# Turning attention rows with VectorE and SBUF transfers instead of TensorE transposes

## The chip, the cores and the metric

The kernel runs on one core of one Trainium2 chip. The metric is the device time in microseconds of one execution, taken as the median of the runs of a kernel. Inputs and outputs are float32. The kernel is one program with its instructions placed on the engines by hand: TensorE (PE), VectorE (DVE), ScalarE (ACT), GpSimd (POOL), and SyncE (SP), which issues all transfers.

## The reference, cut to what matters

One post-norm decoder layer on x of shape (4, 512, 512): a gated slot attention, a cross attention with a context of (4, 512, 128), and a gated feed-forward layer, each followed by a layer norm. The change touches the first of them alone. Each of its 16 heads has keys of 64, values of 128 and 64 slots:

```
q, k, v, g, s = x@Wq, x@Wk, x@Wv, x@Wg, clip(x@Ws, -32, 32)     # per head: 64, 64, 128, 128, 64
z  = cumlogsumexp(s) over time;  p = exp(s - z)
ok[t] = q[t] . sum_{u<=t} k[u] * decayed p[u]                   # a score for each slot
pv[t] = softmax(ok[t]) over the 64 slots
o[t]  = pv[t] . sum_{u<=t} decayed p[u] * v[u]
o = o * rsqrt(mean(o^2) + 1e-5) * g_norm_weight                 # over the 128 values
o = o * g * sigmoid(g)
x = layernorm(x + o.reshape(t, 16*128) @ Wo)
```

The kernel works with e = exp(s), the slot "probabilities" before they are divided by their running sum z, and multiplies by 1/z where it is needed. It needs e twice: with slots on partitions (`eT`, from the projection) and with time on partitions (`e`). It needs the output rows `og` with time on partitions (from the last products) and turned, with the 128 values of a head on partitions (`oT`), as the stationary operand of the product with Wo.

## The kernel before, in words

The attention walks 32 steps n = 4p + j: p is one of 8 pairs of heads, j one of 4 batch elements, each with 512 times in 4 tiles of 128. After 31 of them (n = 0 to 30, all built by one `step` function per engine) comes `last_step` (n = 31), then `output_and_max`, and then the cross attention and the feed-forward layer. Each engine has its own list of instructions, written out in order; engines meet by semaphores alone, so a wait holds up everything behind it on the same engine. TensorE's order sets the shape of a step. In step n it runs, one after the other: the three causal score chunks of n; the projections S and VG of step n+1 (each projection group is 12 matmuls of 512 columns: 4 parts of the inner dimension, 3 products of high and low halves); `slots(n)` (L1131) and `states(n)` (L1103); `out_rows(n)`, 8 transposes of the rows `og` that step n-1 left; the projection VG+1; 4 transposes of the normalised slot scores; `project_out(n)`, 24 matmuls that multiply the turned rows of step n-1 by Wo; 4 transposes of the slot softmax `pv`; the projections VG+2 and VG+3; the diagonal score blocks; the projections Q and K; `transpose_e(n + 1)`, 4 transposes; and `values(n)` (L1144, L1149). All transposes of this part go through `transpose4` and have line L1004 in the profile.

Around this, GpSimd works out the factors of the norm (`factor`) and multiplies the rows by them (`scale_o`, L808). ScalarE copies the turned rows out of PSUM as the rounded high half `oT_hi` (L1554), VectorE makes the low half `oT_lo` (L1820), both with the factor 0.5 times the norm's weight (`gw_half`). VectorE adds each product with Wo to `acc` (`add_out`, L1828), takes slot maxima (L1845), subtracts them (L1850), sums (L1856) and scales (L1860); ScalarE's exponential stands between (L1591). VectorE's `gated_output` (L1873) writes `og` at the end of a step. ScalarE copies the transposed probabilities to `e` (L1559).

SyncE holds only weight loads in this part (L556, L561, L564, L570), five at a time for the next pair and one for Wo. Projections wait for the `gate_ready` count of the projection two groups earlier, so VG+3 waits for the gating of VG+1, Q for that of VG+2. Every product is three matmuls of float32r halves (`mm3`, L66 to L68).

Of the kernel before, what the change touches and what calls it, by code (L numbers as in the profile page):

```python
# [147 lines left out]
def layer_program(nc, x, ctx_in, Wq, Wk, Wv, Wg, Ws, Wo, gw, gate_w, up_w, down_w, gate_s, up_s, down_s, out,  # L148
# [6 lines left out]
    with ExitStack() as ctx:  # L155
        place = {}

        def sb(name, shape, dt=F32):
            place[name] = (nc.sbuf_base + 31) // 32 * 32
            return ctx.enter_context(nc.sbuf_tensor("a_" + name, shape, dt))  # L160
# [5 lines left out]
        def sem(name):  # L166
            return ctx.enter_context(nc.semaphore("a_" + name))
# [24 lines left out]
        og = sb("og", [P, 2 * TT, DV])  # L192
# [5 lines left out]
        oT_hi = sb("oT_hi", [P, 2, T], F32R)  # L198
        oT_lo = sb("oT_lo", [P, 2, T], F32R)
# [51 lines left out]
        oT_done = sem("oT_done")  # L251
        wo_done = sem("wo_done")
# [42 lines left out]
        def each_pair(eng, step):  # L295

            for n in range(NSTEP - 1):
                step(n, n // B, n % B, n == 0)

        def at(n, k):  # L300

            return isinstance(n, int) and n == k
# [270 lines left out]
        def _(sp):  # L573
# [102 lines left out]
        def _(pool):  # L676
# [99 lines left out]
            def split_wo(p):  # L776
                pool.wait_ge(raw_wo_in, (p + 1) * 16)
                split(raw_wo, wo_hi[:, :, :], wo_lo[:, :, :], wo_hi_ready, wo_ready, p + 1)
# [25 lines left out]
            def scale_o(n):  # L804

                wait(pool, fac, FAC * n)
                wait(pool, og_ready, 2 * n)
                nc.gpsimd.tensor_tensor(og[:, :, :], og[:, :, :],  # L808
                                        f1[:, :].rearrange("p (g o) -> p g o", o=1).broadcast_to([P, 2 * TT, DV]),
                                        ALU.mult).then_inc(ogs_ready, 1)  # L810
# [45 lines left out]
            nc.gpsimd.tensor_scalar(gw_half[:, :], gw_half[:, :], 0.5, None, ALU.mult).then_inc(gw_ready, 1)  # L856
            split_wo(0)
# [66 lines left out]
        def _(pe):  # L924
# [182 lines left out]
            def out_rows(n):  # L1107

                wait(pe, ogs_ready, n)
                for h in range(2):  # L1110
                    transpose4(ob[h], [og[:, 2 * t + h, :] for t in range(TT)]).then_inc(oT_done, 1)

            def project_out(n, pair, tiles):

                pe.wait_ge(wo_ready, pair + 1)
                wait(pe, oTlo_ready, 2 * n)
                for t in tiles:
                    if t >= 2:
                        wait(pe, added, 4 * (n - 1) + t - 1)
                    for h in range(2):  # L1120
                        mm = mm3(pe, ob[t % 2], (oT_hi[:, h, t * P:(t + 1) * P], oT_lo[:, h, t * P:(t + 1) * P]),
                                 (wo_hi[:, h, :], wo_lo[:, h, :]), h == 0, h == 1)
                    mm.then_inc(wo_done, 1)
# [34 lines left out]
            def step(n, p, j, first):  # L1158
# [8 lines left out]
                pe.wait_ge(e_ready, n + 1)  # L1167
# [6 lines left out]
                if not first:  # L1174
                    out_rows(n)
# [8 lines left out]
                if at(n, 1):  # L1184
                    transpose_x(3, (0, 1))
                if not first:
# [7 lines left out]
                    if into:  # L1194
                        pe.wait_ge(opsT_ready, 1)
                        transpose_operands(0, 0, 2)
                pe.wait_ge(pv_ready, n + 1)
                transpose4(okb, [pv[:, 2 * t:2 * t + 2, :].rearrange("p h m -> p (h m)") for t in range(TT)])\
                    .then_inc(pvT_done, 1)
                if into:  # L1200
                    pe.wait_ge(opsT_ready, 2)
                    transpose_operands(0, 0, 3)
                next_project(VG + 2)
                if into:
                    pe.wait_ge(opsT_ready, 3)
                    transpose_operands(0, 0, 4)
                    pe.wait_ge(added, 4 * n)
                    max_pair(0, 0)
# [18 lines left out]
                transpose_e(n + 1)  # L1227
# [4 lines left out]
            def last_step(n):  # L1232
                pe.wait_ge(left_ready, 2 * n + 1)
                pe.wait_ge(right_ready, 2 * n + 1)
                pe.wait_ge(e_ready, n + 1)
# [253 lines left out]
        def _(act):  # L1489
# [60 lines left out]
            def copy_oT(n):  # L1550

                for h in range(2):
                    wait(act, oT_done, 2 * (n - 1) + h + 1)
                    nc.scalar.activation(oT_hi[:, h, :], ob[h], ACT.Copy,  # L1554
                                         scale=gw_half[:, 0:1]).then_inc(oThi_ready, 1)
# [17 lines left out]
            def step(n, p, j, first):  # L1573
# [11 lines left out]
                if not first:  # L1585
                    copy_oT(n)
# [5 lines left out]
                if into:  # L1592
                    copy_queries(0, 0, 1)
                    copy_queries(0, 0, 2)
                if at(n, 0) or at(n, 1):
                    high_x(n + 2)
                act.wait_ge(wT_ready, n + 1)
                high_right(wT)
                if into:
                    copy_queries(0, 0, 3)  # L1600
                next_proj(VG + 2)
                if into:
                    copy_queries(0, 0, 4)
# [3 lines left out]
                copy_e(n + 1)  # L1607
# [111 lines left out]
        def _(dve):  # L1719
# [97 lines left out]
            def low_oT(n):  # L1817
                for h in range(2):
                    wait(dve, oThi_ready, 2 * (n - 1) + h + 1)
                    nc.vector.scalar_tensor_tensor(out=oT_lo[:, h, :], in0=ob[h],  # L1820
                                                   scalar=gw_half[:, 0:1], in1=oT_hi[:, h, :].bitcast(F32),
                                                   op0=ALU.mult, op1=ALU.subtract).then_inc(oTlo_ready, 1)
# [43 lines left out]
            def gated_output(n, j):  # L1866
                ob = value_banks(n)
                for half in (1, 0):
                    if half:
                        dve.wait_ge(o_done, n + 1)  # L1870
                    else:
                        dve.wait_ge(sq_done, 2 * n + 1)
                    nc.vector.tensor_tensor(og[:, :, :].rearrange("p (t h) c -> p t h c", h=2)[:, :, half, :],  # L1873
                                            ob[half].rearrange("p (t c) -> p t c", c=DV),
                                            gate[:, j % 2, :, half * DV:(half + 1) * DV], ALU.mult).then_inc(og_ready, 1)

            def step(n, p, j, first):
# [17 lines left out]
                if at(n, 0) or at(n, 1):  # L1895
                    less_maxima(n)
# [6 lines left out]
                if not (at(n, 0) or at(n, 1)):  # L1903
                    less_maxima(n)
# [4 lines left out]
                slot_sum(n)  # L1909
                if not first:  # L1910
                    add_out(n, (j - 1) % B, (2, 3))
                scaled_weights(n)
                slot_reciprocals(n)
                dve.wait_ge(wT_ready, n + 1)
                low_right(wT, 2 * n + 1)
                if norm_now and not into:
                    statistics(n, j - 1)
                gating(n + 1, VG + 2, b1)
# [278 lines left out]
```

## Time and profile before

| | |
|---|---|
| runs of the kernel before | 1991.13, 1991.74, 1994.18 us; median 1991.74 |
| profiled execution, first to last instruction (its time on the page) | 1991.0 us |
| TensorE busy | 1963.5 us, 99% of the span |
| VectorE / ScalarE / GpSimd busy | 1367.6 / 780.5 / 562.7 us |
| attention steps, 30 to 1168 us | 1138 us, TensorE busy 1134 of them, granted clock 1.00 |
| mean granted TensorE clock | 0.995 |

The page adds up what each engine was busy with. It is one execution, a little under the median. Durations of matmuls overlap, because they are pipelined: what a matmul costs is the distance from its start to the next one's start, not its duration. A row of the timeline merges equal neighbours: it gives the start, the duration from the first start to the last end, engine, line, what is written and read, and how many. PEld is the load of the stationary operand, which runs beside the matmul before it. SPq is SyncE issuing a transfer; its duration is that of the issue, not of the transfer.

### The profile page before, as it was taken

How to read it: one execution, taken by the hardware profiler on the slowest of the kernel's cores; microseconds unless marked ns; L12 is line 12 of the kernel's file. 1: busy time of each engine (PE TensorE's matmuls, PEld its weight loads, DVE VectorE, ACT ScalarE, POOL GpSimd, SP SyncE). 2: the span in 40 equal slices, each digit the busy share in tenths (PEclk: the TensorE clock that was granted, in tenths of full speed). 3: DMA queues.
4: the chain of work that ended last, by engine and by line, in shares of the span. 5: the costliest groups of instructions: out<-in, count | busy, mean ns of one | idle time of the engine just before them, and what ended most of it. 6: DMA issues, size and time to landing. Idle time of an engine off the chain costs nothing.

```text
span 1991.0 us, 30723 instructions
## 1 busy us (share of the span) xinstructions
PE 1963.5 (99%) x11879; PEld 1444.2 (73%) x11879; DVE 1367.6 (69%) x2206; ACT 780.5 (39%) x1915; POOL 562.7 (28%) x600
## 2 busy tenths in 40 slices
PE   8999999999999999999999989999999999999998
PEld 7888888878878888888788874444444478888886
DVE  4666666666666666666666778999999865555556
ACT  3332232332332322323323324888888732122123
POOL 2142152152152242242242333244242211111112
PEclk9999999999999999999999998999999999999999
DMA  5000100100001001001000000111110100000002
GB/s 169 1 1 12 38 1 12 38 2 25 24 12 37 2 11 38 1 11 38 1 12 3 6 2 19 30 29 26 26 31 20 34 17 16 32 16 16 31 17 85
DMA packets 58449, 46.89 MB, mean 24 GB/s; under 512 B 14288, under 2 KB 47056, under 8 KB 58320
## 3 DMA queue, kind: packets, MB, share of 16 engines
q1 hardware_dynamic: 58320, 45.11, 7.7%
q8 instruction: 88, 1.44, 0.3%
q14 instruction: 41, 0.34, 0.1%
HBM read 32.78 MB, written 4.19 MB: 19 GB/s over the span
## 4 chain that ended last, share of the span: by engine, by line
PE 94%; ACT 3%; DVE 2%; issue 0%; DMA 0%; POOL 0%; POOLq 0%; DVEq 0%; SPq 0%; ACTq 0%
PE a_ps L66 20%; PE a_ps L68 19%; PE a_ps L67 19%; PE a_ps L988 6%; PE a_ps L950 5%; PE a_ps L1004 4%; PE a_ps L1131 4%; PE a_ps L1144 3%; PE a_ps L972 3%; PE a_ps L1064 2%; PE a_ps L932 2%; PE a_ps L1067 2%; PE a_ps L1070 2%; ACT x_prob L1651 2%; PE a_ps L1149 1%; PE a_ps L1103 1%
## 5 line engine op out<-in xcount | busy, mean ns | idle before, releaser
L1725 DVE TENSOR_REDUCE a_raw_qks<-a_ps 128x1 f32<-128x512 f32 x512 | 321.1, 684 | 16.8 <-PE a_ps L950 15.9
L1651 ACT ACTIVATE x_prob<-a_ps 128x512 f32<-128x512 f32 x512 | 280.7, 611 | 62.9 <-PE a_ps L972 61.4
L66 PE MATMUL a_ps<-a_vg_hi,a_xT_lo 128*128 128x512 f32 x512 | 205.0, 400 | 0.0
L68 PE MATMUL a_ps<-a_vg_hi,a_xT_hi 128*128 128x512 f32 x512 | 199.8, 390 | 0.0
L67 PE MATMUL a_ps<-a_vg_lo,a_xT_hi 128*128 128x512 f32 x512 | 199.6, 390 | 0.0
L1777 DVE SCALAR_TENSOR_TENSOR a_gate<-a_gate,a_ps 128x256 f32<-128x256 f32 x128 | 53.8, 420 | 180.1 <-ACT a_gate L1539 180.1
L783 POOL TENSOR_TENSOR a_causal<-a_causal,a_mask 128x128 f32<-128x128 f32 x32 | 14.7, 458 | 557.7 <-ACT a_causal L1544 557.7
L66 PE MATMUL a_ps<-a_xT_hi,a_qks_lo 128*128 128x512 f32 x384 | 157.5, 410 | 0.4 <-DVE a_xT_lo L1756 0.4
L890 POOL TENSOR_TENSOR f_h_lo<-f_h,f_h_hi 128x512 fp32r<-128x512 f32 x44 | 57.0, 1295 | 334.8 <-ACT f_h_hi L1686 334.8
L68 PE MATMUL a_ps<-a_xT_hi,a_qks_hi 128*128 128x512 f32 x384 | 150.5, 392 | 0.0
L67 PE MATMUL a_ps<-a_xT_lo,a_qks_hi 128*128 128x512 f32 x384 | 149.5, 389 | 0.0
L950 PE MATMUL a_ps<-a_xT_lo,a_xT_hi 64*128 64x512 f32 x384 | 143.4, 461 | 2.3 <-DVE a_raw_qks L1725 1.6
L972 PE MATMUL a_ps<-a_xT_hi,a_xT_lo 64*128 64x512 f32 x384 | 140.7, 452 | 0.6 <-ACT x_prob L1651 0.5
L66 PE MATMUL a_ps<-a_xT_hi,f_gu_lo 128*128 128x512 f32 x352 | 138.3, 393 | 0.0
L68 PE MATMUL a_ps<-a_xT_hi,f_gu_hi 128*128 128x512 f32 x352 | 137.1, 390 | 0.0
L67 PE MATMUL a_ps<-f_xT_lo,f_gu_hi 128*128 128x512 f32 x352 | 137.0, 389 | 0.0
L988 PE MATMUL a_ps<-x_prob,x_values 128*32 128x512 f32 x1024 | 137.0, 608 | 0.0
L950 PEld LDWEIGHTS a_ps<-a_xT_lo,a_xT_hi 64*128 64x128 f32 x384 | 61.2, 188 | 97.4 <-issue 38.8
L1537 ACT COPY a_v<-a_ps 128x256 f32<-128x256 f32 x128 | 47.8, 373 | 207.4 <-PE a_ps L68 207.4
L2053 DVE TENSOR_TENSOR acc<-acc,a_ps 128x512 f32<-128x512 f32 x172 | 115.5, 686 | 8.7 <-PE a_ps L68 8.7
L68 PEld LDWEIGHTS a_ps<-a_vg_hi,a_xT_hi 128*128 128x128 f32 x512 | 96.1, 188 | 20.3
L1828 DVE TENSOR_TENSOR acc<-acc,a_ps 128x512 f32<-128x512 f32 x128 | 87.9, 688 | 31.5 <-PE a_ps L68 23.8
(202 smaller groups left out, 4593.8 us busy)
## 6 DMA issues: line engine op xcount, KB each, us to landing
a_raw_vg<-in_L_attn_Wv_dram SPq DMA_DIRECT2D x8, 512.0 KB, 4.0
a_raw_vg<-in_L_attn_Wg_dram SPq DMA_DIRECT2D x8, 512.0 KB, 6.3
a_raw_qks<-in_L_attn_Wo_dram SPq DMA_DIRECT2D x8, 512.0 KB, 3.7
a_xT_lo<-a_xT_lo SPq DMA_DIRECT2D x32, 128.0 KB, 2.3
x_values<-acc SPq DMA_DIRECT2D x13, 256.0 KB, 2.8
acc<-in_x_dram SPq DMA_DIRECT2D x3, 1024.0 KB, 10.2
out_dram<-acc SPq DMA_DIRECT2D x6, 512.0 KB, 2.8
f_raw_down<-in_L_ffn_down_w_dram SPq DMA_DIRECT2D x11, 256.0 KB, 2.9
```

What stands on the lines that cost most here:

```text
L66: pe.matmul(out, w_lo, x_hi, start=start, stop=False)
L67: pe.matmul(out, w_hi, x_lo, start=False, stop=False)
L68: return pe.matmul(out, w_hi, x_hi, start=False, stop=stop)
L950: pe.matmul(max_bank(u, q, i, par), qs[q][HALF[par], tile, st * P:(st + 1) * P], ks[q][(tile // 2) ^ par][HALF[par], :], start=True, stop= ...
L972: pe.matmul(score_bank(q, s, par), ks[q][g ^ par][HALF[par], t * P:(t + 1) * P], qs[q][HALF[par], 2 * g + pair, :], start=True, stop=True) ...
L988: mm = pe.matmul(avb[32 * i:32 * (i + 1), :], cv[:, q, t, g, :], prob[i % 2][:, (s + i // 2) % 4, :], start=(t == 0), stop=(t == TT - 1))
L1004: last = pe.transpose(bank[:, i * P:(i + 1) * P], src, ident[:, :])
L1131: mm = pe.matmul(okb[DK * h:DK * (h + 1), i * P:T], e[:, i, DK * h:DK * (h + 1)], causal[:, h, KEY_AT[i]:KEY_AT[i] + T - i * P], start=(i ...
L1651: nc.scalar.activation(prob[par][:, s % 4, :], score_bank(q, s, par), ACT.Exp, scale=X_SCALE).then_inc(exp_done[par], 1)
L1725: nc.vector.tensor_reduce(nm[:, q % 2, i % 4, par, i // 4:i // 4 + 1], max_bank(u, q, i, par), AX.X, ALU.max, negate=True).then_inc(max_re ...
L1828: nc.vector.tensor_tensor(a, a, ob[t % 2], ALU.add).then_inc(added, 1)
L2053: nc.vector.tensor_tensor(a, a, down_bank(v, b, t), ALU.add).then_inc(f_added, 1)
```

## The change

Rows and probabilities are no longer turned by TensorE. For the output rows of steps n = 1 to 30, VectorE turns `og` (128x1024) inside its 32x32 blocks in one instruction (`turn_output`); then SyncE issues 16 transfers inside SBUF, each of a block of 32 partitions with 8 runs of 32 words on each, that put the blocks in their transposed places in `oT_raw` (`move_output`), which lies over `oT_lo`. ScalarE copies all of it to `oT_hi` once the 16 have landed (`high_turned`), and GpSimd makes `oT_lo` (`low_turned`). For the probabilities of steps 1 to 31, VectorE turns `eT` (128x512) in the same way into the first half of `og`'s words (`turn_e`), once the 16 transfers that read `og` have landed, and SyncE issues 16 more with 4 runs of 32 words on each partition (`move_e`). `gated_output` waits for these, since it writes `og`. TensorE loses 8 + 4 transposes of a step; steps 0 (for its own `e`), 31 and the last output keep theirs. The factor `gw_half` is now multiplied into Wo by GpSimd (one more 128x1024 instruction for each pair). TensorE's order in a step becomes: chunks, S, VG, slots, states, VG+1, transposes of the scores, VG+2, transposes of `pv`, `project_out` with all four tiles, VG+3, diagonals, Q, K, values. VectorE's order changes with it. The core of the diff (the index views of `og` and the declarations of semaphores are cut; `MOVES` is 16 x 16, `TURNED` is 30):

```diff
-            with sp.Fori(1, PAIRS) as p:
-                sp.wait_ge(wo_ready, p)
-                sp.wait_ge(vg_ready, p)
-                load_s(sp, p)
-                load_vgqk(sp, p)
-                load_output(sp, p)
+            def move_output(n):
+                sp.wait_ge(og_turned, n)
+                wait(sp, wo_done, 4 * (n - 1))
+                for r in range(4):
+                    for c in range(4):
+                        sp.dma_start(oT_raw[32 * c:32 * (c + 1), :, 32 * r:32 * (r + 1)],
+                                     og[32 * r:32 * (r + 1), c, :, :]).then_inc(oT_in, 16)
+            def move_e(m):
+                sp.wait_ge(e_turned, m)
+                sp.wait_ge(states_done, m)
+                for r in range(4):
+                    for c in range(4):
+                        sp.dma_start(e[32 * c:32 * (c + 1), :, 32 * r:32 * (r + 1)],
+                                     og_words[32 * r:32 * (r + 1), P * c:P * (c + 1)]
+                                     .rearrange("p (i r) -> p i r", i=TT)).then_inc(e_in, 16)
+            for n in range(NSTEP - 1):
+                p, j = n // B + 1, n % B
+                if n:
+                    move_output(n)
+                move_e(n + 1)
+                if j == 0 and p < PAIRS:
+                    sp.wait_ge(wo_ready, p)
+                    sp.wait_ge(vg_ready, p)
+                    load_s(sp, p)
+                    load_vgqk(sp, p)
+                if j == 3 and p < PAIRS:
+                    load_output(sp, p)
...
             def split_wo(p):
                 pool.wait_ge(raw_wo_in, (p + 1) * 16)
+                nc.gpsimd.tensor_tensor(raw_wo, raw_wo, gw_half[:, :].rearrange("p (k o) -> p k o", o=1).broadcast_to([P, 2, D]), ALU.mult).then_inc(wo_scaled, 1)
+                pool.wait_ge(wo_scaled, p + 1)
...
+            def low_turned(n):
+                pool.wait_ge(oThi_ready, oT_count(n))
+                nc.gpsimd.tensor_tensor(oT_lo[:, :, :], oT_raw[:, :, :], oT_hi[:, :, :].bitcast(F32), ALU.subtract).then_inc(oTlo_ready, 1)
             def step(n, p, j, first):            # GpSimd
                 if not first:
                     factor(n - 1)
                     scale_o(n)
+                    low_turned(n)
...
             def step(n, p, j, first):            # TensorE
-                pe.wait_ge(e_ready, n + 1)
+                if first:
+                    pe.wait_ge(e_ready, 1)
+                else:
+                    pe.wait_ge(e_in, MOVES * n)
                 states(n, j)
-                if not first:
-                    out_rows(n)
                 next_project(VG + 1)
...
+                next_project(VG + 2)
+                pe.wait_ge(pv_ready, n + 1)
+                transpose4(okb, [...pv...]).then_inc(pvT_done, 1)
                 if not first:
                     project_out(n, pair0, (0, 1))
                     project_out(n, pair0, (2, 3))
-                pe.wait_ge(pv_ready, n + 1)
-                transpose4(okb, [...pv...]).then_inc(pvT_done, 1)
-                next_project(VG + 2)
                 next_project(VG + 3)
...
-                transpose_e(n + 1)
                 values(n, j)
...
+            def high_turned(n):                  # ScalarE, between the copies of VG and of VG+1
+                act.wait_ge(oT_in, MOVES * n)
+                nc.scalar.copy(oT_hi[:, :, :], oT_raw[:, :, :]).then_inc(oThi_ready, 1)
...
+            def turn_output(n):                  # VectorE
+                dve.wait_ge(ogs_ready, n)
+                nc.vector.transpose(og_words, og_words).then_inc(og_turned, 1)
+            def turn_e(m):
+                dve.wait_ge(eT_ready, m + 1)
+                wait(dve, oT_in, MOVES * (m - 1))
+                nc.vector.transpose(og_words[:, 0:T]..., eT[:, :]...).then_inc(e_turned, 1)
             def gated_output(n, j):
+                if n < NSTEP - 1:
+                    dve.wait_ge(e_in, MOVES * (n + 1))
...
             def step(n, p, j, first):            # VectorE
                 gating(n + 1, VG, b1)
+                if not first:
+                    turn_output(n)
                 normalised_slots(n)
                 running_states(n)
-                if not first:
-                    low_oT(n)
-                gating(n + 1, VG + 1, b1)
+                turn_e(n + 1)
                 slot_maxima(n)
+                less_maxima(n)
+                gating(n + 1, VG + 1, b1)
+                slot_sum(n)
+                scaled_weights(n)
+                slot_reciprocals(n)
+                if not at(n, 1):
+                    gating(n + 1, VG + 2, b1)
                 if not first:
                     add_out(n, (j - 1) % B, (0,))
+                dve.wait_ge(wT_ready, n + 1)
+                low_right(wT, 2 * n + 1)
                 if not first:
                     add_out(n, (j - 1) % B, (1,))
                 if not first:
                     add_out(n, (j - 1) % B, (2, 3))
```

## Rows read from the trace of the kernel before

**Rows 1.** the page, busy time of the engines, then the chain that ended last

```profile
PE 1963.5 (99%) x11879; PEld 1444.2 (73%) x11879; DVE 1367.6 (69%) x2206; ACT 780.5 (39%) x1915; POOL 562.7 (28%) x600
...
PE 94%; ACT 3%; DVE 2%; issue 0%; DMA 0%; POOL 0%; POOLq 0%; DVEq 0%; SPq 0%; ACTq 0%
```

**Rows 2.** a whole step: us; busy us and count by engine; clock; DMA share; GB/s

```profile
578.44:614.88 36.44, 36.44 (x236) 29.64 (x234) 22.36 (x35) 11.14 (x35) 11.62 (x11) 1.00 0.05 15
```

**Rows 3.** the timeline of TensorE in one step (start, duration, engine, line, what)

```profile
586.23 2.37 PE L1131 MATMUL a_ps<-a_causal,a_e 128*64 128x512 f32 x16
...
589.19 1.09 PE L1004 MATMUL a_ps<-ident,a_og 128*128 128x128 f32 x8
590.04 0.48 PE L66 MATMUL a_ps<-a_vg_hi,a_xT_lo 128*128 128x512 f32 x1
...
592.88 0.60 PE L1004 MATMUL a_ps<-ident,a_flat 128*128 128x128 f32 x4
593.24 0.47 PE L66 MATMUL a_ps<-a_wo_hi,a_oT_lo 128*128 128x512 f32 x1
...
598.81 0.60 PE L1004 MATMUL a_ps<-ident,a_flat 128*128 128x128 f32 x4
599.17 0.48 PE L66 MATMUL a_ps<-a_vg_hi,a_xT_lo 128*128 128x512 f32 x1
...
604.80 0.33 PE L1064 MATMUL a_ps<-a_right_hi,a_left_lo 64*128 64x128 f32 x2
...
611.88 0.60 PE L1004 MATMUL a_ps<-ident,a_eT 128*128 128x128 f32 x4
612.31 1.95 PE L1144 MATMUL a_ps<-a_v,a_causal 128*128 128x128 f32 x16
...
622.67 2.37 PE L1131 MATMUL a_ps<-a_causal,a_e 128*64 128x512 f32 x16
```

**Rows 4.** the timeline of GpSimd in the same step

```profile
585.90 1.90 POOL L808 TENSOR_TENSOR a_og<-a_og,a_f 128x1024 f32<-128x1024 f32 x1
...
589.73 2.40 POOL L759 TENSOR_TENSOR a_qks_lo<-a_raw_qks,a_qks_hi 128x1024 fp32r<-128x1024 f32 x1
```

**Rows 5.** the timeline of VectorE in the same step

```profile
587.03 0.42 DVE L1777 SCALAR_TENSOR_TENSOR a_gate<-a_gate,a_ps 128x256 f32<-128x256 f32 x1 [0.99 <-ACT a_gate L1539]
...
594.11 0.68 DVE L1845 TENSOR_REDUCE a_mx<-a_ps 128x8 f32<-128x512 f32 x1
...
607.60 1.22 DVE L1784 TENSOR_TENSOR_SCAN a_rz<-a_eT 128x512 f32<-128x512 f32 x1
```

**Rows 6.** the timeline of ScalarE in the next step, a copy from SBUF

```profile
618.15 0.70 ACT L1520 CAST a_left_hi<-a_eT 128x512 fp32r<-128x512 f32 x1
```

**Rows 7.** transfers issued back to back by SyncE inside SBUF

```profile
1200.67 1.10 SPq L618 DMA_DIRECT2D a_xT_lo<-a_xT_lo  x2
1201.88 0.67 SPq L609 DMA_DIRECT2D x_values<-acc  x1
```

**Rows 8.** a load from HBM, issued right behind another

```profile
349.42 0.46 SPq L561 DMA_DIRECT2D a_raw_vg<-in_L_attn_Wg_dram  x1
```

**Rows 9.** the page, transfers by size and median time from issue to landing

```profile
a_xT_lo<-a_xT_lo SPq DMA_DIRECT2D x32, 128.0 KB, 2.3
x_values<-acc SPq DMA_DIRECT2D x13, 256.0 KB, 2.8
```

**Rows 10.** queue, packets, MB, share of 16 engines: 1076 to 1084 us, two context loads

```profile
q1 hardware_dynamic: 1056, 0.13, 10.5%
```

**Rows 11.** the same for 1231 to 1236 us, runs of 2 KB inside SBUF

```profile
q1 hardware_dynamic: 160, 0.26, 23.2%
```

**Rows 12.** stretches around a wait of TensorE in the last step (columns as Rows 2)

```profile
1180.00:1185.00 5.00, 2.91 (x25) 2.29 (x26) 4.67 (x8) 2.15 (x4) 4.92 (x8) 0.98 0.00 0
1185.00:1190.00 5.00, 5.00 (x27) 4.30 (x27) 3.33 (x7) 0.00 (x0) 4.95 (x6) 0.50 0.09 15
1190.00:1195.00 5.00, 5.00 (x35) 4.40 (x35) 1.58 (x3) 1.58 (x13) 0.00 (x0) 0.84 0.01 2
```

More of the change, by code:

```diff
@@ L197, in layer_program @@
         squares = flat.rearrange("p (g c) -> p g c", c=DV).bitcast(mybir.dt.bfloat16)
-        oT_hi = sb("oT_hi", [P, 2, T], F32R)
-        oT_lo = sb("oT_lo", [P, 2, T], F32R)
+        oT_hi = sb("oT_hi", [P, 2 * TT, P], F32R)
+        oT_lo = sb("oT_lo", [P, 2 * TT, P], F32R)
+        oT_raw = over("oT_raw", "oT_lo", [P, 2 * TT, P])
         mask = sb("mask", [P, 5, P])
@@ L251, in layer_program @@
         oT_done = sem("oT_done")
+        og_turned = sem("og_turned")
+        oT_in = sem("oT_in")
+        e_turned = sem("e_turned")
+        e_in = sem("e_in")
+        wo_scaled = sem("wo_scaled")
         wo_done = sem("wo_done")
@@ L298, in each_pair, with oT_count @@
                 step(n, n // B, n % B, n == 0)
+        TURNED = NSTEP - 2
+        MOVES = 16 * 16
+        def oT_count(n, h=1):
+            return n if n <= TURNED else TURNED + 2 * (n - TURNED - 1) + h + 1
         def at(n, k):
@@ L1110, in out_rows @@
                 for h in range(2):
-                    transpose4(ob[h], [og[:, 2 * t + h, :] for t in range(TT)]).then_inc(oT_done, 1)
+                    transpose4(ob[h], [og_rows[:, 2 * t + h, :] for t in range(TT)]).then_inc(oT_done, 1)
             def project_out(n, pair, tiles):
                 pe.wait_ge(wo_ready, pair + 1)
-                wait(pe, oTlo_ready, 2 * n)
+                wait(pe, oTlo_ready, oT_count(n))
                 for t in tiles:
@@ L1120, in project_out @@
                     for h in range(2):
[L1121 removed]
+                        mm = mm3(pe, ob[t % 2], (oT_hi[:, 2 * t + h, :], oT_lo[:, 2 * t + h, :]),
                                  (wo_hi[:, h, :], wo_lo[:, h, :]), h == 0, h == 1)
@@ L1166, in step @@
                 pe.wait_ge(right_ready, 2 * n + 1)
-                pe.wait_ge(e_ready, n + 1)
+                if first:
+                    pe.wait_ge(e_ready, 1)
+                else:
+                    pe.wait_ge(e_in, MOVES * n)
                 into = n == NSTEP - 2
@@ L1185, in step @@
                     transpose_x(3, (0, 1))
+                next_project(VG + 2)
+                pe.wait_ge(pv_ready, n + 1)
+                transpose4(okb, [pv[:, 2 * t:2 * t + 2, :].rearrange("p h m -> p (h m)") for t in range(TT)])\
+                    .then_inc(pvT_done, 1)
                 if not first:
@@ L1585, in step @@
                 if not first:
-                    copy_oT(n)
+                    high_turned(n)
                 next_proj(VG + 1)
@@ L1599, in step @@
                 if into:
[L1600 to L1603, printed above, removed]
+                    for i in range(1, TILES):
+                        copy_queries(0, 0, i)
                 next_proj(VG + 3)
@@ L1818, in low_oT @@
                 for h in range(2):
[L1819 to L1822, printed above, removed]
+                    dve.wait_ge(oThi_ready, oT_count(n, h))
+                    nc.vector.tensor_tensor(oT_lo[:, :, :].rearrange("p (t h) c -> p h t c", h=2)[:, h],
+                                            ob[h].rearrange("p (t c) -> p t c", c=P),
+                                            oT_hi[:, :, :].bitcast(F32).rearrange("p (t h) c -> p h t c", h=2)[:, h],
+                                            ALU.subtract).then_inc(oTlo_ready, 1)
+            def turn_output(n):
[4 more added lines that the diff above has]
+                wait(dve, oT_in, MOVES * (m - 1))
+                nc.vector.transpose(og_words[:, 0:T].rearrange("p (s i r) -> p s i r", s=4, i=TT),
+                                    eT[:, :].rearrange("p (i s r) -> p s i r", i=TT, s=4)).then_inc(e_turned, 1)
             def add_out(n, b, tiles):
@@ L1872, in gated_output @@
                         dve.wait_ge(sq_done, 2 * n + 1)
-                    nc.vector.tensor_tensor(og[:, :, :].rearrange("p (t h) c -> p t h c", h=2)[:, :, half, :],
-                                            ob[half].rearrange("p (t c) -> p t c", c=DV),
-                                            gate[:, j % 2, :, half * DV:(half + 1) * DV], ALU.mult).then_inc(og_ready, 1)
+                    if n < TURNED:
+                        out = og[:, :, :, :].rearrange("p b (t h) r -> p t h b r", h=2)[:, :, half, :, :]
+                    else:
+                        out = og_rows.rearrange("p (t h) (b r) -> p t h b r", h=2, b=4)[:, :, half, :, :]
+                    nc.vector.tensor_tensor(out, ob[half].rearrange("p (t b r) -> p t b r", t=TT, b=4),
+                                            gate[:, j % 2, :, half * DV:(half + 1) * DV]
+                                            .rearrange("p t (b r) -> p t b r", b=4), ALU.mult).then_inc(og_ready, 1)
             def step(n, p, j, first):
```

57 lines of the change are left out of this document (25 added, 32 removed).

## The prediction, made before the changed kernel was run

> **What bounds the kernel now.** Read the page first: TensorE is busy for 1963.5 of 1991.0 us, and 94% of the chain that ended last is TensorE [rows 1]. A whole attention step then shows it more sharply: 36.44 us, TensorE busy in all of them at a granted clock of 1.00, VectorE for 22.36, ScalarE 11.14, GpSimd 11.62, the transfer engines at a share of 0.05 [rows 2]. So an instruction taken from TensorE shortens a step by its distance to the next start, and a new wait of TensorE lengthens it. The third view is TensorE's timeline of one step [rows 3], which gives these distances and the times at which it comes for its operands. From there it is a question of when the other engines deliver, read from their timelines. I work in the absolute times of the step that is shown; it repeats every 36.44 us (586.23 to 622.67, [rows 3]).
>
> **What goes.** The 8 transposes of the rows take 589.19 to 590.04, 0.85 us; the 4 of the probabilities 611.88 to 612.31, 0.43 us [rows 3]. The first go in steps 1 to 30, the second 31 times: 30 x 0.85 + 31 x 0.43 = 38.8 us. That is all that TensorE can gain.
>
> **When TensorE will want what is late now.** Without the row transposes VG+1 starts at 589.19 and ends 2.84 later (590.04 to 592.88), 592.03. The score transposes take 0.36, to 592.39. VG+2 takes half of 599.17 to 604.80, 2.82, to 595.21. There it wants `pv`; its transposes take 0.36 (598.81 to 599.17), and at 595.57 it wants both halves of `oT`. This is 2.33 us later than now (593.24). All from [rows 3].
>
> **When the rows arrive.** It is one serial chain.
> - GpSimd scales the rows until 585.90 + 1.90 = 587.80 [rows 4]. VectorE is free by then (587.03 + 0.42 = 587.45, [rows 5]).
> - VectorE's turn of 128x1024 words: the trace has no transpose on VectorE. An elementwise instruction took 0.42 for 256 columns and 0.68 for 512 [rows 5], so 0.26 for each 256 more: 0.68 + 2 x 0.26 = 1.2. The dearest per column that is near is the scan, 1.22 for 512 [rows 5], so 2.4. I take 1.2, since nothing says that it runs slower than one pass. With the handover it ends at 589.1.
> - 16 transfers, issued one after the other by one queue. The trace has none of 32 partitions. Inside SBUF, issues behind each other are (1201.88 - 1200.67) / 2 = 0.60 apart, and one takes 0.67 by itself [rows 7]; a load from HBM takes 0.46 [rows 8]. I take 0.60, the nearest in kind: the last is issued 15 x 0.60 = 9.0 after the first, at 598.15. It lands 2.3 later (2.8 for the 256 KB one, [rows 9]): 600.45.
> - Do the transfer engines keep up? 1056 packets, nearly all of 128 bytes, were 10.5% of 16 x 8 us, 13.4 us, so 13 ns each [rows 10]. A transfer here is 256 of them and 16 for the semaphore, 17 on each of 16 engines: 0.22 us, under 0.60. So the issue binds, not the bytes.
> - ScalarE's copy of 128x1024: 0.70 for 512 [rows 6], 1.3 for twice that (1.4 at most): 601.8.
> - GpSimd's difference of 128x1024: 2.40 for the same shape [rows 4]: with handovers 604.3.
>
> TensorE wanted it at 595.57: it waits 8.7 us. The output projection was moved by 2.33 us, the arrival by 11.
>
> **What else hangs on the 16.** `turn_e` waits for them on VectorE, and behind it stand the slot maxima, their subtraction, all gatings from VG+1 on, and the additions. 600.45, then the turn of 512 words 0.7, two instructions of 0.68 [rows 5], ScalarE's exponential about 0.70 [rows 6], handovers 0.2: `pv` comes at 603.4, where TensorE wants it at 595.21. So TensorE stands from 595.21, and this wait lies inside the longer one (604.3) with 0.5 us to spare after its 4 transposes. On ScalarE `high_turned` holds the two short copies of VG+1 and the exponential; it is done at 601.8, and the exponential is not asked for before 602.6. On GpSimd `low_turned` holds `split_qk` of the fourth step of a pair (4.3 us, to 608.6); Q starts at 604.3 + 5.57 + 2.82 + 1.48 = 614.2, so it is hidden by 5.6 us. The scaling of Wo, 1.9 us for a pair, is wanted a step later: nothing.
> - SyncE: free at 598.75; `turn_e` ends at 601.2, 16 more issues and a landing, 11.3 us, 612.5. The next step's chunks and `gated_output` want them near 624 (the step's start 578.44, [rows 2], plus 45.7). Hidden by 11 us; 32 issues are 19 us of a queue that is used for about 3 us a pair now. The weight loads queue behind them, with a step or more of slack. If the first 16 were quick and only these slow, nothing would be lost.
> - VectorE loses 1.4 us of `low_oT` and gains 1.9 of turns: nothing, it is not the bound.
>
> **The clock.** TensorE ran every step shown at 1.00. In the last step it had stood idle for 2.09 of 5 us, and the clock then was 0.50 (1.2 GHz) for 0.2 + 5 + 1.6 = 6.8 us, during which TensorE was busy throughout [rows 12]. A wait of 9 us in each step should do the same. While TensorE waits, the half clock costs nothing; I take about half of such a stretch, 3.6 us, to fall after the wait, and half speed loses half of it: 1.8 us a step. Bounds: 0 (it never falls, or is back in time), and 6.8 / 2 = 3.4.
>
> **The sum.** A step with a wait: -1.28 + 8.7 + 1.8 = +9.2 us, to 45.7. Thirty of them: +276.6; step 0 loses 0.43. Against the profiled 1991.0 us this is 2267 us; that execution lies 0.7 under the median of the runs, so I say 2268. Low end: issues 0.46 apart (-2.1) and no clock loss (-1.8), 3.9 x 30 = 117 less: 2150. High end: issues 0.67 and a landing of 2.8 (+1.5), VectorE's turn 2.4 (+1.2), clock 3.4 (+1.6), 4.3 x 30 = 130 more: 2397, widened to 2420 for the second rival.
>
> The Trainium skill, VectorE: DVE Perf Modes, section The three transpose paths, gives 311 ns for a 128x128 bf16 transpose in 32x32 blocks; no row shows one. Eight of these would be 2.5 us, an estimate by that page, and the sum would be 2306.
>
> **Rivals.**
> - *The transfers overlap as if they were one, and the kernel is faster.* For it: the bytes are small, 512 KB, and a single 256 KB transfer inside SBUF lands 2.8 us after its issue [rows 9]. The rows would be there at 592.0, both halves at 595.8, and TensorE would wait 0.2: 1991.0 - 38.8 + 6 = 1958. Place: SyncE's queue. It decides at an arrival 3.9 us after the turn, where the wait eats the 1.28; with 2.3 for the landing this wants issues (3.9 - 2.3) / 15 = 0.11 apart. Against it: no issue in [rows 7, 8] is under 0.46. The Trainium skill's rule says as much as this rival: DMA: Bandwidth & Descriptors, section Anatomy of one DMA, prices a transfer at 2.0 us plus bytes over 436 GB/s with setup and descriptors small; taken for 512 KB that is 3.2 us, and the kernel would take about 1970, an estimate by that page. The rule has no term for one queue issuing 16; the landing of 2.3 agrees with its fixed part. Chance 0.06.
> - *The packets bind.* If a packet of 128 bytes inside SBUF, from 32 partitions to 32 others, took as long as one of 2 KB there (23.2% of 16 x 5 us over 160 packets, 0.116 us, [rows 11]), a transfer would be 17 x 0.116 = 2.0 us, the sixteen 32 us in place of 9.6, and 30 steps 660 us more: up to 2930. Half of that extra is 2600. For it: no row has this kind. Against: the row for 128 bytes says a ninth. It decides from 0.60 / 17 = 35 ns a packet. Chance 0.08.
> - *The wait is there, the clock stays up*: 1.8 x 30 less, 2214. It lies inside the forecast's range.
> - *VectorE holds it up another way*, so that less is lost, or nothing changes: nothing on the page speaks for it. 0.04 in all, of which 0.01 within 0.2%.
>
> **Chances.** The forecast with its bounds 0.82, packets 0.08, overlap 0.06, the rest 0.04. The range 2150 to 2420 leaves out the overlap, most of the packets' case and some of the forecast's own tail. Within 0.2% (4 us) is about what a measurement of this kernel can't tell from no change. Faster 0.06, same 0.01, slower 0.93.
>
> **What would show it.** Right: a step of 44 to 47 us; SyncE's issues about 0.6 apart, 16 in a row twice a step; VectorE's line of `turn_e` waiting near 11 us for a transfer; TensorE idle for 8 to 9 us before the transposes of `pv` and `project_out`, and a granted clock under 1 in every step. Wrong: issues closer than 0.2, or `oT_lo` there when TensorE comes for it. If the wait is right but the clock stays at 1.00, only that term was wrong.

## The result, and the profile after

The changed kernel takes 2301.94 us (median of 4 runs, 2301.11 to 2303.61), the kernel before 1992.72 (1991.13 to 1994.18) on the same chip: a ratio of 1.156, 95% interval 1.154 to 1.157. Forecast were 2268 us and a range of 2150 to 2420: the direction and the mechanism came out, the size 34 us too small. The profiled execution has a span of 2299.4 us.

The page, busy time of the engines and the chain that ended last, as [rows 1]:

```profile
PE 1999.6 (87%) x11515; PEld 1454.8 (63%) x11515; DVE 1369.9 (60%) x2207; ACT 750.8 (33%) x1854; POOL 648.6 (28%) x638
...
PE 59%; SPq 12%; DVE 9%; POOL 8%; ACT 5%; issue 3%; DMA 3%; POOLq 0%; DVEq 0%; ACTq 0%
```

TensorE was 94% of the chain and is 59% now; the largest newcomer is SyncE's queue with 12%. A whole step, from one scaling of the rows on GpSimd to the next, as [rows 2]: 45.73 us where there were 36.44, TensorE busy for 37.12 of them, and a granted clock under 1.

```profile
674.49:720.22 45.73, 37.12 (x220) 29.59 (x219) 25.34 (x36) 10.28 (x33) 19.55 (x13) 0.93 0.12 18
```

The same step on each engine, to be read as one chain: first GpSimd and VectorE, as [rows 4, 5],

```profile
674.49 1.91 POOL L857 TENSOR_TENSOR a_og<-a_og,a_f 128x1024 f32<-128x1024 f32 x1
690.60 2.35 POOL L863 TENSOR_TENSOR a_oT_lo<-x_oT_raw,a_oT_hi 128x1024 fp32r<-128x1024 f32 x1 [14.20 <-ACT a_oT_hi L1610]
```

```profile
676.44 1.25 DVE L1877 STREAM_TRANSPOSE a_og<-a_og 128x1024 f32<-128x1024 f32 x1 [0.46 <-POOL a_og L857]
...
689.55 0.71 DVE L1882 STREAM_TRANSPOSE a_og<-a_eT 128x512 f32<-128x512 f32 x1 [10.45 <-DMA x_oT_raw<-a_og]
```

then the issues of SyncE, as [rows 7], and ScalarE, as [rows 6],

```profile
677.71 10.40 SPq L607 DMA_DIRECT2D x_oT_raw<-a_og  x16
690.29 10.83 SPq L616 DMA_DIRECT2D a_e<-a_og  x16
```

```profile
689.48 1.04 ACT L1610 CAST a_oT_hi<-x_oT_raw 128x1024 fp32r<-128x1024 f32 x1 [13.95 <-DMA x_oT_raw<-a_og]
...
691.60 0.63 ACT L1646 ACTIVATE a_flat<-a_flat 128x512 f32<-128x512 f32 x1 [0.52 <-DVE a_flat L1911]
```

and TensorE, as [rows 3]: behind VG+2 it stands for 8.33 us, until the exponential gives it `pv`. (The profile counts this from the modelled end of the last matmul, 683.56 + 0.39; counted from where the next one could have started, 683.56 + 0.23, it is 8.49.) Then come 4 transposes and the output projection, whose first starts are 0.43 apart where at full clock they are 0.23.

```profile
683.56 0.39 PE L68 MATMUL a_ps<-a_vg_hi,a_xT_hi 128*128 128x512 f32 x1
692.28 1.11 PE L1060 MATMUL a_ps<-ident,a_flat 128*128 128x128 f32 x4 [8.33 <-ACT a_flat L1646]
693.10 0.77 PE L66 MATMUL a_ps<-a_wo_hi,a_oT_lo 128*128 128x512 f32 x1
693.66 0.63 PE L67 MATMUL a_ps<-a_wo_lo,a_oT_hi 128*128 128x512 f32 x1
694.09 0.63 PE L68 MATMUL a_ps<-a_wo_hi,a_oT_hi 128*128 128x512 f32 x1
...
696.18 0.40 PE L67 MATMUL a_ps<-a_wo_lo,a_oT_hi 128*128 128x512 f32 x1
696.41 0.40 PE L68 MATMUL a_ps<-a_wo_hi,a_oT_hi 128*128 128x512 f32 x1
```

The waits of TensorE summed over the span (us in total, times, longest) show the two places that matter. One is the wait for `pv` in 29 steps; the other comes once, in step 30, 26.2 us in one piece, and the prediction did not have it.

```profile
PE a_ps L1060 <- ACT a_flat L1646: 242.4, 29, 9.5
PE a_ps L988 <- POOL a_raw_qks L761: 26.2, 1, 26.2
```

How that one comes about is on GpSimd's and SyncE's timelines. In step 30 GpSimd casts the operands of the cross attention, which TensorE turns ahead of VG+2. These casts now stand behind `low_turned`, and behind that GpSimd waits 9.05 us more for a context load, since SyncE issues that load only behind 16 + 16 moves.

```profile
1427.88 2.34 POOL L863 TENSOR_TENSOR a_oT_lo<-x_oT_raw,a_oT_hi 128x1024 fp32r<-128x1024 f32 x1 [14.18 <-ACT a_oT_hi L1610]
...
1440.10 2.04 POOL L734 TENSOR_TENSOR a_raw_vg<-acc,a_zero 128x512 fp32r<-128x512 f32 x2 [9.05 <-DMA a_raw_qks<-in_ctx_dram]
```

```profile
1415.01 10.39 SPq L607 DMA_DIRECT2D x_oT_raw<-a_og  x16
1427.57 10.24 SPq L616 DMA_DIRECT2D a_e<-a_og  x16
1437.86 1.14 SPq L651 DMA_DIRECT2D a_raw_qks<-in_ctx_dram  x2
```

The books by the starts of GpSimd's scaling: from n = 1 to n = 30 a step took 36.54 us on average before and 46.21 after, 29 x 9.66 = 280; the stretch from n = 30 to n = 31 43.3 before and 73.6 after, 30.3 more. That is 310 of the 308 us by which the spans differ.

### The profile page after: what moved, and what is told of

The parts are those of the page before. It is cut to its first block, busy times and chain, and to the rows that moved or that the text cites. A ratio compares the mean times of both kernels' runs of the same rounds, so it can differ in the third digit from the quotient of the medians.

```text
span 2299.4 us, 30948 instructions
## 1 busy us (share of the span) xinstructions
PE 1999.6 (87%) x11515; PEld 1454.8 (63%) x11515; DVE 1369.9 (60%) x2207; ACT 750.8 (33%) x1854; POOL 648.6 (28%) x638
## 4 chain that ended last, share of the span: by engine, by line
PE 59%; SPq 12%; DVE 9%; POOL 8%; ACT 5%; issue 3%; DMA 3%; POOLq 0%; DVEq 0%; ACTq 0%
PE a_ps L66 12%; SPq L607 12%; PE a_ps L67 12%; PE a_ps L68 12%; PE a_ps L1044 5%; PE a_ps L1006 4%; DMA x_oT_raw<-a_og 3%; POOL a_og L857 3%; PE a_ps L1028 2%; POOL a_f L844 2%; PE a_ps L1200 2%; PE a_ps L1060 2%; DVE a_og L1877 2%; PE a_ps L988 2%; ACT x_prob L1701 1%
## 5 line engine op out<-in xcount | busy, mean ns | idle before, releaser
L1060 PE MATMUL a_ps<-ident,a_flat 128*128 128x128 f32 x256 | 53.3, 346 | 243.9 <-ACT a_flat L1646 242.4
L1882 DVE STREAM_TRANSPOSE a_og<-a_eT 128x512 f32<-128x512 f32 x31 | 22.0, 711 | 317.0 <-DMA x_oT_raw<-a_og 317.0
L1060 PEld LDWEIGHTS a_ps<-ident,a_flat 128*128 128x128 f32 x256 | 38.0, 175 | 260.9 <-ACT a_flat L1646 254.6
L863 POOL TENSOR_TENSOR a_oT_lo<-x_oT_raw,a_oT_hi 128x1024 fp32r<-128x1024 f32 x30 | 70.6, 2355 | 429.3 <-ACT a_oT_hi L1610 429.3
L1610 ACT CAST a_oT_hi<-x_oT_raw 128x1024 fp32r<-128x1024 f32 x30 | 31.3, 1044 | 420.1 <-DMA x_oT_raw<-a_og 420.1
L1889 DVE TENSOR_TENSOR acc<-acc,a_ps 128x512 f32<-128x512 f32 x128 | 87.8, 687 | 99.7 <-PE a_ps L68 98.9
```

Of the source, the lines that this page charges most:

```text
L863: nc.gpsimd.tensor_tensor(oT_lo[:, :, :], oT_raw[:, :, :], oT_hi[:, :, :].bitcast(F32), ALU.subtract).then_inc(oTlo_ready, 1)
L1060: last = pe.transpose(bank[:, i * P:(i + 1) * P], src, ident[:, :])
L1889: nc.vector.tensor_tensor(a, a, ob[t % 2], ALU.add).then_inc(added, 1)
```

## The experiments

Each experiment ran beside the kernel before, which took 1993.01 us beside the first four of them, 1991.53 beside the next four and 1990.42 beside the last; the ratios and their 95% intervals are against these. All but `only_e` start from the changed kernel.

**Half of the issues to a second queue** (`two_queues`): is it the number that one queue issues?

```
 move_output (SyncE):    for r in range(4):   ->   for r in range(2):
 high_turned (ScalarE), ahead of its copy:
+    act.wait_ge(og_turned, n); wait(act, wo_done, 4 * (n - 1))
+    for r in (2, 3): for c in range(4): act.dma_start(oT_raw[...], og[...])
```

> ScalarE issues 8 of the 16 row transfers of a step, SyncE the other 8; nothing else changes. Theory (one queue's serial issue is what TensorE waits for; 16 issues took 10.40 us in the changed kernel, 0.65 each): the rows land 8 x 0.65 = 5.2 us earlier in 30 steps, so 2302 - 156 = 2146 us, and down to 2100 if the shorter wait keeps the clock up. Rival (the transfer engines, or landing, set the time, and who issues doesn't matter): 2302, unchanged.

2147.61 us, 1.078 (1.076 to 1.080). The timelines of ScalarE's and SyncE's queues show the two groups side by side, and in this step GpSimd's wait for the high half is 9.31 where it was 14.20:

```profile
655.33 5.51 ACTq L1613 DMA_DIRECT2D x_oT_raw<-a_og  x8
```

```profile
655.33 5.17 SPq L607 DMA_DIRECT2D x_oT_raw<-a_og  x8
```

```profile
663.34 2.35 POOL L863 TENSOR_TENSOR a_oT_lo<-x_oT_raw,a_oT_hi 128x1024 fp32r<-128x1024 f32 x1 [9.31 <-ACT a_oT_hi L1616]
```

Same packets and same bytes, half the time from the first issue to the last: the issue binds. The mean step fell by 5.02 us (46.21 to 41.18). The clock did not stay up: with 3.5 us of waiting for `pv` in a step (101.7 over 29) it was 0.96 in nearly every whole step, so the way down to 2100 stayed closed.

**A quarter of the transfers** (`four_moves`), and **a quarter of the packets** (`quarter_runs`): number against size. Both kernels leave out three quarters of the rows, so they do not compute the layer, and only their time counts.

```
 four_moves:    for c in range(4):  ->  for c in (r,):
 quarter_runs:  oT_raw[32 * c:32 * (c + 1), 0:2, ...], og[..., c, 0:2, :]
 both: oT_hi and oT_lo are made from v, so that all is written
```

> Leaves out 12 of the 16 row transfers of each step (the halves are then taken from other data of the same shape, so only the time means something). Theory: 12 x 0.65 = 7.8 us less of issue in each of 30 steps, nearly the whole wait, and the clock's loss of about 1.6 us with it: 2302 - 30 x 9.4 = about 2020 us. What is left over 1992 is the 26 us wait of step 30. Rival (the wait of TensorE is set by turn_e or by the copies on ScalarE and GpSimd, not by the issues): well above 2100.

2022.28 us, 1.015 (1.014 to 1.017). The loss of the steady steps is nearly gone: a step takes 36.86 us on average, 0.3 more than before the change, and TensorE never waits over 1.8 us for `pv`. Step 30 still takes 65.7 us where it took 43.3, and that is 22 of the 29 us that are left.

> All 16 row transfers stay, but each carries 2 of its 8 runs (a quarter of the packets and bytes; the halves are taken from other data of the same shape). Theory (issue bound): 2302 within 10 us. Rival (packets of 128 bytes bind): a good part of the 10.4 us goes, down to about 2100 us.

2284.35 us, 1.147 (1.145 to 1.148). Twelve issues fewer gave back 280 us, a quarter of the bytes and packets in the same 16 issues 17.6. That is more than the 10 us that I had allowed for. GpSimd's timeline has the rows 0.4 us earlier in each step (a wait of 13.79 against 14.20 in the steps shown, 13.9 against 14.3 on average): SyncE's 16 issues took 0.23 less, and the last landing 0.19 less. The packets count, but little.

```profile
685.41 2.35 POOL L863 TENSOR_TENSOR a_oT_lo<-a_v,a_oT_hi 128x1024 fp32r<-128x1024 f32 x1 [13.79 <-ACT a_oT_hi L1610]
```

**The wait filled with work** (`warm`): what is the clock's share?

```
 step (TensorE), behind VG+2:
+    if not first and not into:
+        keep_clock(70)      # 70 transposes of ident, read by nobody
```

> 70 transposes of the identity into an unused bank while TensorE waits for pv in steps 1 to 29, 0.11 us each at full clock, so 7.5 us of a wait of 8.3. Theory: the granted clock stays at 1.00 and the 1.6 to 1.8 us that the slow stretch after the wait costs in a step come back: 2302 - 29 x 1.7 = 2253 us. Rival (the clock's loss is hidden by the additions on VectorE, or the next step starts late for another reason): 2302.

2279.56 us, 1.144 (1.142 to 1.146): 22 us less, not 49. The clock did stay up in 24 of the 29 steps (1.00 in whole steps, first fence); in the other five it was 0.96, and a part of the projection ran at half clock. The starts on TensorE, averaged over the 29 steps, show where the rest of the gain went. The output projection took 6.23 us in place of 7.47, where it takes 5.5 with nothing in its way; and it began 10.06 us behind the start of VG+2's last matmul in place of 9.57, so 0.49 was lost again there.

The 0.49 is the rows': GpSimd's wait was 14.8 on average (444.2 over 30) in place of 14.3, and SyncE's 16 row issues took 10.89 in place of 10.51. Most groups take 10.40 in both kernels, and a few up to 11.6 (second fence); over 10.6 were 19 of 30 here and 6 of 30 in the changed kernel. In the projection itself a new wait came up in 7 of the 29 steps, those in which GpSimd splits the weights of Q and K: TensorE came to the fourth tile before VectorE had made room, and waited 1.03 us. One instruction of VectorE took 2.46 there in place of 0.69, beside GpSimd's `L799` (third to fifth fence).

```profile
709.58:755.06 45.48, 43.87 (x293) 36.16 (x291) 24.57 (x36) 10.19 (x33) 12.61 (x11) 1.00 0.16 30
```

```profile
667.33 11.52 SPq L607 DMA_DIRECT2D x_oT_raw<-a_og  x16
```

```profile
730.47 2.46 DVE L1819 TENSOR_TENSOR a_right_lo<-a_flat,a_right_hi 128x512 fp32r<-128x512 f32 x1
```

```profile
729.99 2.40 POOL L799 TENSOR_TENSOR a_qks_lo<-a_raw_qks,a_qks_hi 128x1024 fp32r<-128x1024 f32 x1
```

```profile
733.59 0.50 PE L66 MATMUL a_ps<-a_wo_hi,a_oT_lo 128*128 128x512 f32 x1 [1.03 <-DVE acc L1891]
```

So this kernel measures what keeping the clock up is worth here (0.74 a step), not what the half clock takes by itself. Whether the longer groups of issues have to do with TensorE's work was not tried.

**Step 30 as it was** (`end_as_before`): does the missing piece sit there?

```
-TURNED = NSTEP - 2
+TURNED = NSTEP - 3      # step 30: rows and e by TensorE, projection in its old place
```

> Step 30 alone is built as in the kernel before (rows and probabilities turned by TensorE, operands of the cross attention where they were, no transfers of its own, so that the context loads no longer stand behind them); steps 1 to 29 as in the changed kernel. Theory: step 30 of the changed kernel took 73.6 us against 43.3 before, by GpSimd's scale instructions, 30 us more than it had to: 2302 - 30 = 2272 us. Rival (the 26 us wait comes from something later, the cross attention's start): 2302, or the wait turns up elsewhere.

2272.92 us, 1.141 (1.140 to 1.143): 29 us less, all of it in that step (n = 30 to 31 took 43.3 again, the mean of the others 46.20). What is left is the loss of steps 1 to 29. Forecast for these alone were 2268 - 9.2 = 2259 us, so 14 are missing there.

**Only the rows moved** (`only_rows`): `transpose_e` and `copy_e` are back, `turn_e` and `move_e` gone.

```
-                turn_e(n + 1)
-                move_e(n + 1)
+                transpose_e(n + 1)    # TensorE, and copy_e on ScalarE
```

> Rows moved by transfers as in the changed kernel, probabilities turned by TensorE and copied by ScalarE as before: no turn_e on VectorE, 16 issues fewer. Theory (the rows' chain through ScalarE and GpSimd paces a step, turn_e's wait lies inside it): the wait moves from the pv transposes to the output projection and stays about as long, 31 x 0.43 us come back on TensorE, 0.4 to 0.8 a step and part of step 30's 26 us go: 2270 to 2305 us. Rival (turn_e holding VectorE, and so pv, is what paces it): about 8 us a step less, near 2060.

2300.41 us, 1.155 (1.153 to 1.157): within 0.1% of the whole change, so in this kernel the moves of `e` neither gain nor lose beside the rows'. The 0.43 of the 4 transposes came back to TensorE, but its wait for `pv` is 0.6 shorter a step (waits, first line), and it stands 0.33 for `oT_lo` instead. The mean step was 46.40, 0.2 more. Step 30's one wait was 17.1 in place of 26.2, as the context loads have 16 issues fewer ahead of them: they have landed when `low_turned` ends, and GpSimd casts at once (fourth line). Even so its casts begin 19.2 us after the step's scaling of the rows (1418.52), where in the kernel before they begin 2.7 after it (1132.72, second fence), and the step takes 64.6 us in place of 43.3. So of the 30.3 that step 30 loses in the changed kernel about 21 come from the place of the casts behind `low_turned`, and 9 from the queue.

```profile
PE a_ps L1059 <- ACT a_flat L1643: 225.8, 29, 9.0
PE a_ps L987 <- POOL a_raw_qks L760: 17.1, 1, 17.1
PE a_ps L66 <- POOL a_oT_lo L862: 9.7, 29, 0.3
...
1437.73 2.04 POOL L733 TENSOR_TENSOR a_raw_vg<-acc,a_zero 128x512 fp32r<-128x512 f32 x2
```

```profile
1135.40 2.04 POOL L694 TENSOR_TENSOR a_raw_vg<-acc,a_zero 128x512 fp32r<-128x512 f32 x2
```

**Only the probabilities moved** (`only_e`), from the kernel before, with 30 of the 31 moves:

```
+            def turn_e(m):  ...      # VectorE, behind low_oT, into og
+            def move_e(m):  ...      # SyncE, 16 issues, into e
-                transpose_e(n + 1)   # steps 0 to 29
-                copy_e(n + 1)
```

> The kernel before, with only the probabilities of steps 1 to 30 turned by VectorE and moved by 16 transfers; rows by TensorE as before, output projection where it was. Theory (the 16 issues and the landing, 12.7 us, lie inside 25 us of slack to the next step): TensorE loses 30 x 0.43 us, so 1993 - 13 = 1980 us. Rival (the wait on the transfers comes to lie at the start of the next step or at gated_output): 1993 or more.

1981.85 us, 0.995 (0.994 to 0.997): **faster** than before, by 0.5%. These are as many issues of the same queue, and they are hidden, since their result is wanted only in the next step. The mean step is 36.19, 0.35 under 36.54; 0.43 was taken out.

**The projection late enough** (`late`): both moves, but the output projection between Q and K, about 7.4 us later in TensorE's work than in the changed kernel (9.8 later than in the kernel before); 4 of the 16 row moves on ScalarE; `high_turned` and `low_turned` further back in the lists of ScalarE and GpSimd; `turn_e` behind the slot weights; step 30 as before.

```
 TensorE:  next_project(Q)
+          project_out(n, pair, range(TT))
           next_project(K)
 VectorE:  inverse_z(n + 1)            # the scan, then a reciprocal
+          add_out(n, b, (0,))
           low_right(...)
+          add_out(n, b, (1, 2, 3))
```

> Both kinds of move, ordered by what the traces say of their arrival: output projection between Q and K (wanted 24.2 us after the step's start), turn_e behind the slot weights, 12 row transfers issued by SyncE and 4 by ScalarE, step 30 as before. Theory: rows land 19.8 us after the step's start, both halves are there at 24.3, so all transposes taken from TensorE count: 1993 - 29 x 1.28 = 1956 us, and up to 1970 with small waits. Rival (another wait takes the place of the first: the additions at the end of the step, ScalarE's issues before its copies): 1990 to 2020.

1982.34 us, 0.995 (0.994 to 0.996): faster than before by 0.5%, but 12 us slower than the upper end that I gave. The waits for the rows are gone (0.8 us in the whole span); in their place the third tile of the projection waits for `add_out(0)` (0.32 in the timeline, 29 times), since both use the same bank of PSUM. VectorE's timeline says why: the scan ahead of it took 2.46, beside `low_turned`.

```profile
634.08 2.46 DVE L1955 TENSOR_TENSOR_SCAN a_rz<-a_eT 128x512 f32<-128x512 f32 x1
636.57 1.75 DVE L1958 RECIPROCAL a_rz<-a_rz 128x256 f32<-128x256 f32 x1
638.24 0.63 DVE L2010 TENSOR_TENSOR acc<-acc,a_ps 128x512 f32<-128x512 f32 x1
```

```profile
633.05 2.41 POOL L863 TENSOR_TENSOR a_oT_lo<-x_oT_raw,a_oT_hi 128x1024 fp32r<-128x1024 f32 x1 [12.41 <-ACT a_oT_hi L1690]
```

**The additions ahead of the reciprocal** (`late2`, from `late`):

```
 VectorE:  the scan of inverse_z
           low_right(...)
+          add_out(n, b, (0, 1))
           the reciprocal of inverse_z
+          add_out(n, b, (2, 3))
```

> The kernel `late` with one edit on VectorE: the first two additions of the output projection go ahead of the reciprocal of the slot sums, behind the scan. In the trace of `late` the step was 35.88 us (36.44 before the change, 35.2 hoped for), and the one wait of TensorE that came back in 29 steps was that of the third tile of the output projection for the first addition: 0.32 each, the project_out stretch 6.15 us long in place of 5.57. Theory (this order on VectorE is all that was missing): 29 x 0.58 = 17 us less, about 1965 us (1962 to 1970). Rival (the delay only moves: the reciprocal ends 1.3 us later, or the scan at 2.46 us keeps the additions late all the same): 1976 us or more.

1965.52 us (1963.76 to 1965.95), 0.987 (0.985 to 0.989): 1.3% faster than before, the fastest of all here. The scan is still 2.46; nobody waits behind it now. In a whole step TensorE is busy throughout, at full clock, for 35.25 us in place of 36.44 [rows 2]: all but 0.1 of the 1.28 that the change takes out.

```profile
609.65:644.90 35.25, 35.25 (x222) 28.34 (x220) 23.90 (x36) 10.28 (x33) 14.54 (x13) 1.00 0.30 67
```

## Why the prediction was right, and what it missed

**The chain of the rows: right.** From the end of the scaling to `oT_lo` 16.5 us were forecast; 676.40 to 692.95 are 16.55. By terms: the turn 1.25 (1.2 forecast); the issues 10.40 / 16 = 0.65 apart (0.60), the last 9.75 after the first (9.0); the landing 2.0 (2.3); ScalarE's copy 1.04 (1.3); GpSimd's difference 2.35 (2.40). The issues cost 0.75 more than forecast, landing and copy 0.56 less, and these nearly cancel.

**The wait of TensorE: right.** It stood for 8.49 us before `pv`, counted as the forecast counts (8.2), and the output projection began 9.31 us after the end of VG+2 (9.09). Of the 0.5 us that `pv` was to have to spare nothing was left: the forecast had its 4 transposes at full clock, and at half clock they took 0.82 in place of 0.36 and ended at 693.10, behind `oT_lo` at 692.95. So in the changed kernel TensorE never stands for `oT_lo` in these steps, and the two chains end level. `only_rows` shows it: with `turn_e` gone `pv` came earlier, and the projection began no earlier.

**The clock: right in size, in part by luck.** Forecast were 1.8 us a step after the wait, from a stretch whose half was a guess. In the step shown 7 starts took 693.10 to 696.18, 3.08 where 1.70 are due at full clock (0.33 + 6 x 0.228), so 1.4; in the step before it the half clock lasted to 651.35, and 12 took 5.24 for 2.84, so 2.4. The mean is 1.9, over all 29 steps too (the projection takes 7.47 from its first start to VG+3's, and 5.5 at full clock). The transposes of `pv` lost 0.46 more, which the sum holds in the wait, so the half clock lasted longer behind the wait than the 3.6 us that were taken. That it is lost time does not mean it can be had: `warm` got 0.74 of it.

**The step: 9.2 forecast, 9.66 measured.** In the forecast's terms, averaged over the 29 steps: -1.28 + 9.0 + 1.9 (8.7 and 1.8 forecast). Over 29 steps the shortfall is 13 us.

**Step 30: missed, 21 us.** What failed is that step 30 was counted as one of thirty, and with it two sentences. One is on GpSimd: `low_turned` was looked at for `split_qk` alone, which is hidden; in step 30 it holds the casts of the cross attention's operands, and TensorE comes for these ahead of VG+2. The other is on SyncE, "The weight loads queue behind them, with a step or more of slack": what is true of the weights (a pair ahead) isn't of the context loads, which come on the same queue in that step with GpSimd waiting. Forecast was +9.2, measured +30.3; by `only_rows` about 21 of these come by the first way and 9 by the second, and `end_as_before` took 29 us off in all. The forecast had followed each engine through the steady step alone. 13 + 21 = 34 us is the whole miss.

**The rivals.** Overlap of the transfers (1958 us) fell: 0.65 between issues against the 0.11 that it needed. By the Trainium skill's formula (DMA: Bandwidth & Descriptors, Anatomy of one DMA) the sum was about 1970. It is stated there for one transfer, issued by GpSimd; its fixed part of about 2.0 us agrees with the landing of SyncE's transfers here (medians of 2.0 us for 32 KB each and 1.8 for 16 KB in the profile's list), while 15 issues ahead of the last are outside it. Binding packets fell too: with a quarter of them `quarter_runs` gained 17.6 us of 309. The clock that stays up (2214) was excluded by the 0.93 above; and `warm`, which held it up in most steps, shows that even then more than half of the gain would have been lost to other waits and a few slow stretches. The estimate of 2306 us by the Trainium skill's page VectorE: DVE Perf Modes (The three transpose paths) comes near the measured time for a wrong reason: the turn took 1.25, half of its 2.5.

**The change's own cover: as forecast.** The moves of `e` and VectorE's added work cost the steady step nothing beyond the rows' own wait; `only_e` shows that by itself this part was a gain of 10 us. The change failed by its place in time: it moved the projection by 2.33 us for rows that came 11 later. Another 7.4 us, less of the issue by one queue, step 30 as before and the additions in order on VectorE made 309 us of loss into 25 of gain. What each of the first three, made at once in `late`, is worth in that kernel was not tried.

## What to carry to other kernels

A transpose taken from the busiest engine and split over many small transfers costs the sum of its issues before its landing; count issues times their spacing on one queue, then move the consumer by that much, or split the issues over two queues. When a queue gets a new tenant, go through all that it carries in the first and last steps too, not only in the steady one; and do the same for the list of each engine that gets a new wait. After a wait is removed, look for the next late one: here it was a bank of PSUM, freed behind an instruction that another engine had slowed.

## What the runs showed of the hardware

- The distance between issues of one queue inside SBUF, 32 partitions each, was 0.65 us (10.40 for 16), and 0.69 on ScalarE's (5.51 for 8); with a quarter of the packets still 0.64. Single gaps of up to 2.1 us occur among them, and why is open. Two queues side by side kept their rates.
- VectorE's instructions with two operands in SBUF took longer beside GpSimd's, and by how much depends on when that one ends. The scan is 1.22 alone [rows 5]. In `late` GpSimd's instruction ends at 635.46 and the scan 1.08 later, at 636.54. In the changed kernel's pair with weights to split, the fence below, GpSimd's ends at 708.99 and the scan at 710.07, again 1.08 later. So it is in all 28 slow scans of `late` and all 14 of the changed kernel. This is what the Trainium skill says (SBUF — State Buffer, SBUF: two separate sides): whichever starts first holds the port that they share for its whole instruction, and the other stands until then. The traces agree.

```profile
705.69 4.38 DVE L1834 TENSOR_TENSOR_SCAN a_rz<-a_eT 128x512 f32<-128x512 f32 x1
```

```profile
705.39 3.60 POOL L797 TENSOR_TENSOR a_vg_hi<-a_raw_vg,a_zero 128x2048 fp32r<-128x2048 f32 x1
```

- VectorE turned 128x1024 words in blocks in 1.25 us and 128x512 in 0.71, about the price of an elementwise pass (0.68 for 512 columns, [rows 5]).
- After a wait of 8.3 us with TensorE idle the granted clock was 0.50 (1.2 GHz) for the first 3 us of the projection in one step (fence below), and for 5 in the one before. The same wait full of transposes left it at 1.00 in 24 of 29 steps. With waits of 3.5 us on average (`two_queues`) whole steps were still at 0.96.

```profile
693.00:696.00 3.00, 3.00 (x9) 2.35 (x8) 1.08 (x3) 0.62 (x1) 0.00 (x0) 0.50 0.15 22
696.00:700.00 4.00, 4.00 (x18) 3.29 (x18) 2.66 (x4) 0.00 (x0) 0.00 (x0) 0.99 0.18 28
```
